# The second feed-forward layer of ten token blocks as seven half products instead of eight, inside the attention

## What is computed

```python
def ffn(x):                       # x: tokens x 256
    h = concatenate([x, -x], -1)
    h = relu(s0 * (h @ sign(k0))) * 2      # 512 -> 1024
    h = relu(s1 * (h @ sign(k1))) * 2      # 1024 -> 1024, the layer that is changed
    return s2 * (h @ sign(k2))             # 1024 -> 256

x = x + 0.5 * ffn(layernorm(x))
x = x + attention(layernorm(x))   # 16 heads of 16 features, softmax, projections with biases
x = x + 0.5 * ffn(layernorm(x))
```

## Time and profile before

| | us |
|---|---|
| median of 3 runs | 1525.23 |
| lowest and highest | 1523.41, 1525.33 |
| the profiled execution, span | 1521.2 |
| TensorE busy | 1512.4 (99%) |
| ScalarE busy | 1129.3 (74%) |
| VectorE busy | 574.2 (38%) |

### The profile page before, as it was taken

One profiled execution on the slowest core, in us unless ns is written; L12 is line 12 of the kernel. 1 busy time (PEld: TensorE's weight loads), 2 busy tenths in 40 slices (PEclk: granted clock), 3 DMA queues, 4 the chain that ended last, 5 costly groups with the idle time before them and its releaser, 6 DMA issues.

```text
span 1521.2 us, 31574 instructions
## 1 busy us (share of the span) xinstructions
PE 1512.4 (99%) x12471; PEld 606.1 (40%) x12471; DVE 574.2 (38%) x1298; ACT 1129.3 (74%) x1654; POOL 59.7 (4%) x65
## 2 busy tenths in 40 slices
PE   9999999999999999999999999999999999999999
PEld 5555455334334333333333334334333334334354
DVE  7645764511431243234332333242241332323462
ACT  3221222888889988898989989889988988988721
POOL 2010011001000100010100000000000000000000
PEclk9999999999999999999999999999999999999999
DMA  4122223212331231232223123111213212311110
GB/s 139 42 84 51 75 80 113 71 51 81 84 73 41 96 95 40 67 113 63 81 53 95 40 53 94 39 49 59 81 39 67 82 51 65 104 41 21 47 28 16
DMA packets 110139, 101.46 MB, mean 67 GB/s; under 512 B 55846, under 2 KB 95526, under 8 KB 109990
## 3 DMA queue, kind: packets, MB, share of 16 engines
q1 hardware_dynamic: 109158, 98.60, 23.0%
q10 hardware_dynamic: 832, 0.79, 0.2%
HBM read 61.87 MB, written 25.43 MB: 57 GB/s over the span
## 4 chain that ended last, share of the span: by engine, by line
PE 99%; DVE 0%; ACT 0%; issue 0%; POOL 0%; POOLq 0%
PE psum L888 31%; PE psum L850 30%; PE psum L872 16%; PE psum L750 12%; PE psum L762 3%; PE psum L738 3%; PE psum L769 2%; PE psum L782 1%; PE psum L688 0%; PE psum L775 0%; DVE xn L972 0%; DVE h_lo L982 0%; PE psum L710 0%; DVE x_sb L987 0%; ACT xn L911 0%
## 5 line engine op out<-in xcount | busy, mean ns | idle before, releaser
L942 ACT ACTIVATE prob<-psum 128x512 f32<-128x512 f32 (+1 forms) x1438 | 1016.6, 784 | 120.1 <-PE psum L872 115.4
L888 PE MATMUL psum<-prob,v_sb 128*17 128x512 f32 x4096 | 489.4, 595 | 0.0
L872 PE MATMUL psum<-q_st,k_st 64*128 64x512 f16 x2048 | 350.1, 379 | 0.2
L915 ACT ACTIVATE h_hi<-psum 128x512 f16<-128x512 f32 x183 | 109.6, 604 | 215.8 <-PE psum L750 164.6
L980 DVE TENSOR_SCALAR h_hi<-psum 128x512 f16<-128x512 f32 x73 | 50.5, 692 | 433.8 <-PE psum L850 433.8
L982 DVE SCALAR_TENSOR_TENSOR h_lo<-psum,h_hi 128x512 f16<-128x512 f32 x256 | 169.0, 688 | 86.9 <-ACT h_hi L915 84.4
L888 PEld LDWEIGHTS psum<-prob,v_sb 128*17 128x17 f32 x4096 | 95.3, 96 | 262.9 <-issue 166.4
L872 PEld LDWEIGHTS psum<-q_st,k_st 64*128 64x128 f16 x2048 | 82.5, 94 | 279.1 <-ACT prob L942 210.7
L850 PE MATMUL psum<-h_hi,w 64*128 64x512 f16 x1184 | 152.1, 376 | 0.2 <-ACT h_hi L915 0.2
L850 PE MATMUL psum<-h_lo,w 64*128 64x512 f16 x1184 | 152.0, 376 | 0.0
L750 PE MATMUL psum<-h_hi,w 128*128 128x512 f16 x432 | 102.5, 380 | 2.2 <-DVE h_lo L982 2.2
(11 more groups left out here) (109 smaller groups left out, 860.0 us busy)
## 6 DMA issues: line engine op xcount, KB each, us to landing
k_st<-k_halves SPq DMA_DIRECT2D x64, 512.0 KB, 4.4
q_halves<-piece SPq DMA_DIRECT2D x32, 256.0 KB, 2.5
q_st<-q_halves SPq DMA_DIRECT2D x64, 128.0 KB, 4.8
x_rows<-x_sb SPq DMA_DIRECT2D x16, 256.0 KB, 2.2
k_halves<-piece SPq DMA_DIRECT2D x16, 256.0 KB, 2.8
att_rows<-o_sb SPq DMA_DIRECT2D x128, 32.0 KB
x_sb<-x_rows SPq DMA_DIRECT2D x8, 512.0 KB, 4.0
att_t<-att_rows SPq DMA_DIRECT2D x16, 256.0 KB
```

What stands on the lines that cost most here:

```text
L872: mm = pe.matmul(psum[:, score_bank[h + r], :], k_st[rows, slot, t * P:(t + 1) * P], q_st[rows, slot, :], start=True, stop=True)
L888: mm = pe.matmul(psum[32 * j:32 * j + va, O_BANK, :], v_sb[:, b * key_tiles + t, GROUP * g4 + j, :], prob[:, h % PROBS, :], start=(t == 0) ...
L915: act.activation(hi, psum[:, bank, :], ACT.Relu).then_inc(act_done, 1)
L942: act.activation(prob[:, to:to + count, :], psum[:, bank:bank + count, :], ACT.Exp, scale=score_scale / QK_SCALE ** 2).then_inc(exp_sem, 1)
```

## The change

For the blocks u = 5 to 14 (`SEVEN`) l2 is computed by the Winograd form of Strassen's method. The 1024 x 1024 weights are cut into four quarters and the 1024 x 512 activations into four quarters of 512 x 256; seven products of quarters (`PRODUCTS`) take the place of eight. A product is run as two halves of 2 output tiles (step kind `p`), 14 a block, each of 2 x 8 matmuls of 256 columns, or 16 pairs in the attention (16 slots a step, `(8, 8)`).

- The three sums and the difference of the weights are made once (`w1` gets seven quarters): three by GpSimd at the start, one (S3) by GpSimd after l2 of block 4, which overwrites a quarter, and it is undone near the end (`pool_w3`).
- The sums of the activations are made by VectorE. In these blocks l1 is read from PSUM with one ReLU into f32 scratch (`sums`, or `den_t` and `att_t`), by VectorE alone. Then, for each of four pairs of tiles: `plain` (a copy to f16 and the rest to f16, 768 columns each), `sums` (four additions of 256 columns) and `summed` (copy and rest, 1024 columns each). They lie in their own queue and go into the steps after l1 by `lay_sums`.
- The products of one bank follow each other in it: after 1 comes 2, after 6 come 7 and 4, after 5 comes 3. TensorE starts the later one only when the earlier was read (`BEFORE`). VectorE reads each product (in the tail ScalarE reads 1 and 2) and, where an output is finished, hi and lo are made from f32 in SBUF (`low`).
- The order is new. The attention begins before l1 of block 5: in the ten blocks l1 of the next block comes before l3 (but in u = 14), so l1 of block 5 and l3 of block 4 are now inside the attention. l3 takes 13 slots a step instead of 16, and so 5 steps instead of 4. `norm` is cut into `stat` and `norm`; in a product's step the long work may take 0.6 of a step. The projection `out` and the layer norm that follows it lie before product 9 of 14 (12 of 14 in the last block, u = 14).
- To make room in SBUF, the keys have one place instead of two, loaded in halves; the values of a block are written to DRAM by a new DMA and `v_st` holds those of one group. In the second step of a group SyncE loads the second half of its keys and values (three DMAs), in the sixth the first half of the next group's.

```diff
+PRODUCTS = {
+    1: (A11, B11, True, None, (1, 0), (0, 1)),
+    2: (A12, B21, False, 0, (2, 0), (0, 2)),
+    6: (S2, T2, True, None, (0, 1), (0, 1)),
+    7: (S3, T3, False, None, (0, 1), (0, 1)),
+    4: (A22, T4, False, 2, (1, 1), (0, 2)),
+    5: (S1, T1, True, 3, (1, 1), (0, 2)),
+    3: (S4, B22, False, 1, (1, 1), (0, 2)),
+}
+BEFORE = {2: 1, 7: 6, 4: 7, 3: 5}
+SEVEN = range(5, 15)
...
+    def products(u):
+        order = ((1,), (2, -2), (6,), (7,), (4, -4), (5, -5), (3, -3))
+        return [[Step("p" if k > 0 else "low", u, 8 * half + abs(k)) for k in ks]
+                for half in range(2) for ks in order]
...
+        norm_at, merge_at, project_at, square_at = (3, 5, 7, 8) if u in SEVEN else (2, 4, 6, kh)
+        for i, product in enumerate(second):
...
+            if project and i == (12 if last else 9):
                 steps += project + norm_turn(2, ahead)
+            if last and i in (0, 2):
+                steps += divide[2 * i:2 * i + tpb]
+            steps += product
+            if not last and i in (2, 7 if early else 5):
+                steps += divide[tpb * (i > 2):][:tpb]
...
+        if u < qblocks or ahead is None or last:
+            steps += third_layer(u)
...
+        else:
+            steps += first_layer(ahead) + third_layer(u)
...
-    while not (side[0].kind == "l2" and side[0].u == qblocks + 1):
+    while not (side[0].kind == "l1" and side[0].u == qblocks + 1):
...
-    PAIRS = {"l1": (4, 4), "l2": (5, 3), "l3": (10, 6), "qk": (1, 1), "v": (2, 2), "out": (2, 2)}
-    LONG = {"norm": 1.0, "xn": 0.3, "split": 0.4, "flip": 1.0, "merge": 0.4, "heads": 0.26, "peak": 0.3}
+    PAIRS = {"l1": (4, 4), "p": (8, 8), "l3": (8, 5), "qk": (1, 1), "v": (2, 2), "out": (2, 2)}
+    LONG = {"stat": 0.45, "norm": 0.6, "split": 0.4, "flip": 0.6, "merge": 0.4, "heads": 0.26, "peak": 0.3, "xn": 0.33}
+    SUMS_LONG = {"plain": 0.38, "sums": 0.33, "summed": 0.39}
...
+        lay_sums({"l1": 0.72, "l3": 0.8}.get(side[0].kind, math.inf))
+        if not to_sum:
+            lay_long(0.6 if side[0].kind == "p" else math.inf)
...
+    at = [(s.kind, s.u, s.m) for s in side].index(("p", SEVEN[-1], 8 + 6))
+    side[at:at] = waiting
...
+                    if j == 0 and product in BEFORE:
+                        before = find["p", u, 8 * half + BEFORE[product]]
+                        wait_held(before)
...
+        def dve_sums(s):
+            u, j = s.u, s.m
+            b = halves_of_pair(j)
...
+                dve.tensor_copy(h0_hi[:, 0:3, j, :], b[:, 0:3]).then_inc(summed, 1)
+                dve.tensor_tensor(h0_lo[:, 0:3, j, :], b[:, 0:3], h0_hi[:, 0:3, j, :], ALU.subtract).then_inc(summed, 1)
...
-                    if s.u % group_steps == 0:
-                        g = s.u // group_steps
-                        if g + 1 < groups:
-                            sp_stage(g + 1)
+                    g, step = divmod(s.u, group_steps)
+                    if step == 0 and g + 1 < groups:
+                        sp_stage_q(g + 1)
+                    if step == 1 and g:
+                        sp_stage_keys(g, 1)
+                    if step == group_steps // 2 + 1 and g + 1 < groups:
+                        sp_stage_keys(g + 1, 0)
...
+                elif s.kind == "v" and m == 1:
+                    sp.wait_ge(dve_done, s.dve)
+                    sp.dma_start(v_dram[b, :, :, at * run:(at + 1) * run].rearrange("g p c -> p g c"),
+                                 v_new[:].rearrange("p g t c -> p g (t c)")).then_inc(v_out, 16)
```

More of the change, by code:

```diff
@@ L46 @@
     free_exp: int = 0
+    act0: int = 0
+    dve0: int = 0
+    sums: int = 0
     mate: object = None
@@ L131, in norm_turn @@
     def norm_turn(kind, u):
-        steps = [Step("norm", u, kind), Step("xn", u, kind)]
+        steps = [Step("stat", u, kind), Step("norm", u, kind), Step("xn", u, kind)]
         if kind == 1 or u:
@@ L258, in lay_long, with lay_sums @@
             lay(waiting.pop(0), SHARED, False)
+    def lay_sums(most):
+        while to_sum and SUMS_LONG[to_sum[0].kind] <= most:
+            most -= SUMS_LONG[to_sum[0].kind]
+            lay(to_sum.pop(0), SHARED, False)
     def lay_pair(slots):
         s, t = side[0], side[1]
+        if s.kind == "p":
+            if not s.n:
+                s.on_act = False
+                numbers.lay_both(s, SHARED)
+                find[s.kind, s.u, s.m] = s
+                s.hi = 0
+            lo, s.hi = s.hi, s.hi + slots
+            work.append(replace(s, lo=lo, hi=s.hi, mate=s))
+            if s.last():
+                del side[0]
+            return
         if not s.n:
             for bank in (s, t):
-                bank.on_act = bank is t and t.kind in ("l1", "l2", "qk")
+                bank.on_act = bank is t and t.kind == "qk"
                 numbers.lay(bank, SHARED)
@@ L273, in lay_pair, with in_group @@
             work.append(replace(t, lo=t.n, hi=t.n))
+            if s.kind == "l1":
+                to_sum.extend(Step(kind, s.u, s.m) for kind in SUMS)
             del side[0:2]
+    def in_group():
+        return side[0].n or side[0].kind == "p" and not PRODUCTS[side[0].m % 8][2]
     taken = []
@@ L324, in build @@
         if n == 0:
-            lay_pair(8)
+            lay_pair(sum(PAIRS[side[0].kind]))
         if columns and not side[0].n:
@@ L343, in build @@
         lay(held.pop(0), SHARED, False)
-    lay_long(math.inf)
-    if side[0].n:
-        lay_pair(2 * side[0].n - side[0].hi)
-    assert not columns
+    while in_group():
+        lay_pair(side[0].n - side[0].hi if side[0].kind == "p" and side[0].n else 16 if side[0].kind == "p" else 64)
+        lay_idle(att_steps)
+    assert not columns and not to_sum and all(s.kind == "heads" for s in waiting)
+    at = [(s.kind, s.u, s.m) for s in side].index(("p", SEVEN[-1], 8 + 6))
+    side[at:at] = waiting
     work.append(Step("att_end"))
@@ L399, in build @@
     merge_no = {u: no for no, u in enumerate(s.u for s in work if s.kind == "merge")}
+    v_no = {u: no for no, u in enumerate(s.u for s in work if s.kind == "v" and s.m == 1 and s.last())}
     splits_before, squares_read, splits, last_qk = {}, {}, 0, None
@@ L796, in ready_after, with pe_product @@
             return 2 * tpb * out_no(u) + tpb + per_bank * (m + 1)
+        def pe_product(s):
+            u, (half, product) = s.u, divmod(s.m, 8)
+            weights, operand, starts = PRODUCTS[product][:3]
+            if s.lo == 0:
+                if s.free_act:
+                    pe.wait_ge(act_done, s.free_act)
+                if s.free_dve:
+                    pe.wait_ge(dve_done, s.free_dve)
+            for i in range(s.lo, s.hi):
+                turned, j = divmod(i, kh)
+                low, k = divmod(j, kh // 2)
+                if turned and j == 0:
+                    pe.wait_ge(halves, changes_before[s.mm] + 2)
+                if half == 0 and not turned:
+                    wait_operand(u, product, low, k)
+                for tile in range(2):
+                    r = (tile + turned) % 2
+                    rows = slice(64 * r, 64 * r + 64)
+                    mm = pe.matmul(psum[:, SHARED[tile], 0:HALF],
+                                   w1[rows, weights, k, (2 * half + tile) * P:(2 * half + tile + 1) * P],
+                                   (h0_hi, h0_lo)[low][rows, operand, k, :], start=(starts and i == 0), stop=(i == s.n - 1),
+                                   skip_group_check=True)
+                    if i == s.n - 1:
+                        mm.then_inc(mm_done, 1)
+                    elif not turned and j == kh - 1:
+                        mm.then_inc(halves, 1)
         def pe_pair(s):
```

488 lines of the change are left out of this document (370 added, 118 removed).

## The result

The changed kernel takes 1565.5 us (median of 4, 1563.9 to 1567.8) where the kernel before, run beside it, takes 1524.4 (1523.4 to 1525.3): a ratio of 1.0271, 95% interval 1.0257 to 1.0286. It is slower by 41 us. The forecast was 21 us slower, 1546: the measured time lies above the forecast's own range, which ends at 1562, and inside the range for 8 in 10, which ends at 1566, by half a microsecond.

A forecast was written before the change was run, and what follows sets the result against it. TensorE's own program bounds the kernel. Before the attention -8.4, in it +17.1, tail +12.4: together +21.1, span 1542.3, plus 4.0 for the median, 1546 us; own range 1534 to 1562, 8 in 10 1503 to 1566.

The forecast's parts named there:

- Columns: Ten blocks' l2: 224 units of 256 columns instead of 256 per block, 3.4 us a block, -34.2 us.
- loads of weights bind: Rival: weight loads no longer hide, so 256-column pairs take as long as 512-column ones; about 1780 us, chance 0.02.
- it doesn't do what it says: Rival: the products save no columns, a quarter more loads and readings at the same length; above 1550 us, chance 0.03.
- Ahead of the attention: Before the first scores: -14.0 for work moved out, +3.9 for a TensorE stand, +1.7 for the clock, -8.4 us.
- the term of 1.7 for the clock: Half speed after each of five long stands (start, two flips, two in the tail), 1.7 us each, +8.5 us.
- VectorE: Sums and readings stay hidden beside TensorE; VectorE grows about 28 us a block, to some 830 us or 54%.
- The tail: After the last values: two long stands, behind four heads (6.3) and the layer norm (7.8); +9.0 instead of -5.1 us.
- Cover holds: Rival: the order hides flips, loading and layer norm, so only columns and small prices count; 1504 us, chance 0.17.
- only the tail: Rival: flips land in time and the clock stays up apart from the tail's old drop; 1528 us, chance 0.14.
- The flip: In SyncE's queue behind stores and key loads, delaying l1: 4.9 us each for u = 7 and 11, 0.3 for 12; +10.1.
- l3: With 13 slots a step, changes between halves fall inside a run: 0.26 us twice for each of ten blocks, +5.2 us.
- Product steps: In the attention, each product step pays 0.06 us at the change between its two portions, 129 times, +7.7 us.

The follow-up runs named there:

- the best order: Changed kernel with SyncE flips before key loads, tail side work spread, block 15 heads later, long-work limit 0.75, block 3 merge earlier, GpSimd weight difference later: 1516.3 us.
- thin rests: Changed kernel with the remainders (lo) of sums and plain copies made for 2 columns of each 128 only: 1565.4 us.
- long work at 0.75: Changed kernel with long work allowed 0.75 of a product's step instead of 0.6: 1545.6 us.
- the flips first: Changed kernel with only SyncE's order altered: flips of a group's second or third step go before its key and value loads, some also before the stores: 1543.7 us.

## Why the prediction was right and wrong

**Right.** What bounds the kernel, the sign, and the places: all of the stands forecast are there, with the releasers that were named. That the time fell inside the range for 8 in 10, by half a microsecond, was luck: two of four executions lie above 1565.5, one of them above 1566, and the forecast's own range was passed by 3.5 us.
- Columns: pairs of 256 columns still start 0.109 us apart, a product step is 4.61 us long (4.60 forecast). The two rivals "loads of weights bind" and "it doesn't do what it says" are out: with 1516.3 for the best order the saving is real. The rule of the Trainium skill that was weighed in the prediction ("TensorE: Matmul & The Clock Gate", "LDWEIGHTS (loading the stationary operand)") was read there as two loads one after the other, which would have made these steps bound by their loads; the trace disagrees with that reading after the change too: a load's span is 94 ns for the estimated 107, and the two loads of a pair start within 4 ns of each other and run side by side, every 0.109 us. The section itself gives the duration of one load.
- Ahead of the attention -8.5 (-8.4): the stand is 3.85 where 3.9 was worked out. Two of its parts cancel: the last load needed for the first scores was issued 3.0 us after the store of v had landed, not 2.4, and landed after 4.2, not 4.8. That the term of 1.7 for the clock came out was luck. The drop after the stand falls into the attention's first steps, and the 1.6 lost ahead of it are another drop in the first 16 us of the kernel (granted clock 0.72 from 10 to 16 us, where it is 1.00 in the kernel before).
- VectorE: 28.0 us more a block, as forecast, and no bound (thin rests). The total is 854; the 830 of the prediction does not follow from its own 28 a block (574 + 280). The addition of 256 columns takes 0.42 (0.43 taken), the copy of 768 columns 0.95.
- The tail: l1 of 15 at E + 52.05, where 47.8 + 3.4 was forecast; both long stands within 0.5 us.
- "Cover holds" and "only the tail": the cover does not hold in this order. But orders exist in which most of it holds: the best reached 1516, 12 us above that rival's 1504.

**Wrong: sizes in the attention.** The excess over the sum is 18.7 us of span (1561.0 to 1542.3), and nearly all of it lies in these terms:
- *The flip*, +7.7: 21.3 instead of 10.1 + 3.4 for the clock. The issue time was right to 0.2 us. The landing was not: 6.2 to 6.4 us behind three loads of 256 KB and more, not 4.3; l1 of 13 also stood, by 4.4 with half speed where 0.3 was forecast. The upper bound of this term, 18, was there for just this reason; I took the median over all flips for one which my own count had placed right behind the loads, though the trace of the kernel before had two in that place, at 8.0 and 9.0 us.
- *The first heads of block 15*, +3.4, not foreseen: they were laid into step 253, before their softmax sums had arrived. `den_t` lands at 1450.33, and step 254 takes 8.0 us:

```profile
1450.33 0.95 DVE L1487 RECIPROCAL den_t<-den_t 128x128 f32<-128x128 f32 x1 [6.00 <-DMA den_t<-den_rows]
...
1453.45 0.61 PE L1041 MATMUL psum<-h_hi,w 64*128 64x256 f16 x8 [3.23 <-DVE sums L1368]
```

- *l3*, +2.5: its five steps take 21.75 a block, not 21.5.
- *Product steps*, +1.3: 0.07 instead of 0.06, 129 times.
- *u = 8*, +1.8: the stand of the heads is 2.02 (forecast 2.1), but half speed follows it, and the step is 3.9 too long. The merge came out at 1.15 for 1.2.
- The tail, +0.9. Some 1.3 more I find in no single term of the sum; single steps such as 119 (5.14 us) hold part of it.

Of these the flip is the main one, shown by two runs: one removes all three late flips (21.3 us by the steps), the other two of them in another way (16.8). The clock is spread over these terms and was too small in sum: TensorE is busy for 28.3 us in the stretches at the lower level, so half of that, 14.2 us, was lost, for 8.5 forecast. The first scores, two flips and the tail cost 9.1 of it; l1 of 13, step 112 and the first 16 us, 1.7 each, had not been foreseen.

## What to carry to other kernels

A saving on the engine that bounds must be paid for by order: list for each thing that engine needs what stands ahead of it in every strictly ordered queue, in the place where it falls, since the same flip cost 0 or 8 us depending on the step of the group in which it came. When a transfer is placed right behind others, take its landing from rows in the same place of the queue, not the median of all. Before a piece of work is moved, ask what it was covering: moving merge and projection took 3.0 of the 3.8 us of the start at the price of 1.6 elsewhere, while moving l3 uncovered 12.8 us of sums.

## What the runs showed of the hardware

- A small VectorE operation between SBUF tiles can be held until a GpSimd elementwise operation ends: 2.54 us for 0.16, while in the same 4 us an addition that reads PSUM (0.69) and an aggregation (0.38) ran at full pace. The Trainium skill, "SBUF — State Buffer", section "SBUF: two separate sides", says that the two engines share a pair of ports by an exclusive lock held for the whole instruction; the trace agrees for the scaling. The skill limits this to certain VectorE operations, which the two that ran on unharmed don't contradict.
- Half speed does not follow a stand by its length alone: it came after 2.02 us in step 112, and not after 3.23 us at 1453.45 (granted clock 1.00 from 1450 to 1456), nor after 2.52 us in the best order. The same stand differs from kernel to kernel: that of step 112 was followed by half speed in the change and with long work at 0.75, not with the flips first, though l1 of 8 no longer stood in either of the last two; that of step 254 (2.9 to 3.3 us) was not in the change and was in those two. Windows over step 112, with long work at 0.75 and with the flips first (granted clock 0.88 and 1.00):

```profile
774.00:788.00 14.00, 11.98 (x90) 5.99 (x84) 5.83 (x12) 8.14 (x12) 0.00 (x0) 0.88 0.10 27
```

```profile
776.00:790.00 14.00, 11.98 (x122) 6.35 (x120) 6.38 (x16) 9.93 (x15) 0.00 (x0) 1.00 0.17 36
```

The kernel before differs even with itself: its executions have a span of either 1519.3 to 1519.6 or 1521.0 to 1521.5 us, at a mean granted clock of 1.000 or 0.999, which fits its one drop of 1.7 us coming in some and not in others. What decides was not settled.
- The transposing DMA holds SyncE's queue for 1.4 to 5.8 us, 3.18 and 4.26 in the two cases shown, so that what stands behind it is late as well. Its landing, 4.2 to 4.5 us after its start ahead of the attention, with nothing just before it, is 5.6 to 8.1 directly behind three loads.
